# A selective-scan block and an expert network on one core: the convolution's weights and the first norm set up ahead of the other weights

## The chip, the core and the metric

The kernel runs on one core of a Trainium2 chip. A time is device microseconds (us) of one execution. The engines of the core work side by side and meet through semaphores: TensorE (PE, matmul; PEld is its weight load), VectorE (DVE), ScalarE (ACT), GpSimd (POOL), and SyncE (SP), which issues most of the DMAs.

## The reference, cut to what matters

For each of 32 sequences of 256 positions and 128 channels a selective scan is computed on the normed input, and then a gated network of 8 experts (the best 2 of 8 per position, 176 features each) and a shared part of 352 features:

```python
u = silu(conv4(W_in_u @ norm(x)) + conv_b)            # 256 channels, 4 taps
g = u @ W_gate.T                                      # 64 low-rank, 16 b, 16 c
delta = softplus(g[:64] @ W_delta.T + delta_bias)
h = exp(A * delta) * h + (delta * u) * b              # 256 channels x 16 states, along time
y = (sum(h * c) + D * u) * silu(o)                    # o = W_in_o @ norm(x)
x = x + y @ W_out.T
x = x + experts(norm(x)) + shared(norm(x))
```

## The kernel before, in words

**Steps.** All engines run the same loop of steps, k = -3 to 34 (`steps`, L309), each through its own `body`, which is an order written out by hand. A step works on several sequences at once; `on(lag)` says that sequence k + lag exists. In step k, sequence k + 3 is read and its mean and variance are taken; k + 2 is normed, transposed, convolved and gets its `u`, its `g` (L1044, copied to `g_sb` by L579) and `z` (L1083, copied to `z_sb` by L612); k + 1 gets softplus (L553), the products `dd` (delta in its one half by L563, delta times u in the other by L790) and the gate of the output (L513); k goes through the scan; k - 1 gets the second norm; k - 2 goes through the experts.

**The scan of one sequence.** The 256 x 16 states are 8 groups q = 0 to 7 of 128 partitions x 1024. SP spreads `dd` to four times as many partitions by eight DMAs (`rep`, L357, four for each half of the channels), and fetches `b` and `c` for all partitions (`bc`, L336) after a small store (`bc_rows`, L364). For each group ACT makes the decays with four exponentials (L489), POOL the `inject` (L410), DVE scans (L687), and then POOL, or DVE for groups 0 and 4 (L699), multiplies by c (`read`, L420), and PE sums the states (L894). Each of these is a queue of its own in fixed order, with waits on the others.

**Before the steps.** SP issues x of sequence 0 and 13 loads of weights, among them W_in, the taps, and four of 16-byte pieces for A_log (L325). DVE and PE wait for all of them; DVE scales W_in by the taps (L642), PE transposes that and the other weights (L866 to L875, 19 transposes), and DVE and ACT copy the results out, some as two parts, a rounded one and its rest (L650, L665). The transposed weights lie in `decay_ps`. Every engine waits for the last weight before its first `body`. ACT also issues the loads of the experts' weights (L457), into the tiles `state` and `read`, which the scan needs later; ACT rounds them (L534, L535) and DVE takes the rest (L793, L795), both inside step -1. POOL builds a selection matrix `csel_rows` in `rep0` (L388 to L393), which DVE copies (L645).

## Time and profile before

| | us |
|---|---|
| median of 3 runs | 1240.33 |
| the runs | 1239.35 to 1240.44 |
| profiled execution, its own time | 1238.7 |
| its span | 1237.0 |

Busy in the span: PE 1123.3 us (91%), POOL 1067.5 (86%), DVE 1066.9 (86%), ACT 1011.0 (82%). The page cuts the span into 40 slices of 31 us; all engines are at seven tenths or more from the third slice on, and below that in the first two. So the table tells of two things: a long stretch in which four engines share the load, and a start. A timeline row gives the start, the duration of the whole merged row, the engine, the line, the operation with its tiles, and in brackets the idle time before it with what ended it.

### The profile page before, as it was taken

The numbers are of one execution on the slowest core, as the hardware profiler recorded it, in microseconds if no ns is written. First come the engines' busy times: TensorE is split into PE (matmuls) and PEld (weight loads), VectorE is DVE, ScalarE is ACT, GpSimd is POOL, SyncE is SP. The second block draws the span as 40 slices with busy tenths as digits, with TensorE's granted clock in tenths as the row PEclk, the third lists the DMA queues.
The fourth block names the chain that finished last, engine by engine and source line by source line (L and its number), as shares of the span: only waits on it lengthen the run. The fifth ranks groups of instructions, "written<-read, shape, count | busy, mean of one in ns | idle before, by whom it ended". The sixth has DMA issues, their size and how long they took to land. (4 is left out here: it accounts for less than half of the span.)

```text
span 1237.0 us, 25691 instructions
## 1 busy us (share of the span) xinstructions
PE 1123.3 (91%) x9075; PEld 919.1 (74%) x9075; DVE 1066.9 (86%) x1700; ACT 1011.0 (82%) x2119; POOL 1067.5 (86%) x502
## 2 busy tenths in 40 slices
PE   3456999999999999999999999999999999998887
PEld 2334778878778787887787878877878788876676
DVE  3277899999999999999998999999999999999854
ACT  2778888888888888888988888889888988897642
POOL 3299899999999999999998999999999999999810
PEclk8767999999999999999999999999999999999899
DMA  4444433344434333444343334443433344434000
GB/s 119 109 111 105 102 84 85 107 109 109 99 92 112 87 82 101 109 109 113 79 113 86 82 101 109 108 112 80 113 94 83 93 109 110 107 79 103 5 6 9
DMA packets 71482, 115.05 MB, mean 93 GB/s; under 512 B 8174, under 2 KB 30395, under 8 KB 71355
## 3 DMA queue, kind: packets, MB, share of 16 engines
q1 hardware_dynamic: 67178, 110.71, 35.0%
q10 hardware_dynamic: 4176, 2.70, 0.8%
q8 instruction: 72, 1.18, 0.4%
q14 instruction: 56, 0.45, 0.1%
HBM read 41.04 MB, written 5.24 MB: 37 GB/s over the span
## 5 line engine op out<-in xcount | busy, mean ns | idle before, releaser
L410 POOL TENSOR_TENSOR inject<-rep,bc 128x1024 f32<-128x1024 f32 x256 | 604.6, 2384 | 20.2 <-DMA rep<-dd 20.2
L420 POOL TENSOR_TENSOR read<-state,bc 128x1024 f32<-128x1024 f32 x192 | 452.2, 2376 | 10.2 <-DVE state L687 8.8
L687 DVE TENSOR_TENSOR_SCAN state<-decay_ps,inject 128x1024 f32<-128x1024 f32 x192 | 432.0, 2279 | 13.8 <-ACT decay_ps L489 13.0
L489 ACT ACTIVATE decay_ps<-rep,neg_a 128x255 f32<-128x255 f32 x1024 | 427.0, 465 | 8.9 <-DVE state L687 3.5
L936 PE MATMUL acc_ps<-ffn_down,features 128*128 128x128 f32 (+1 forms) x1792 | 244.8, 281 | 0.5 <-DVE features L716 0.5
L936 PEld LDWEIGHTS acc_ps<-ffn_down,features 128*128 128x128 f32 (+1 forms) x1792 | 220.3, 192 | 23.4 <-DVE features L716 7.4
L902 PE MATMUL work_ps<-xn2T_part,ffn_gate 128*128 128x256 f32 x1344 | 219.4, 300 | 6.7 <-ACT g_silu L476 3.0
L476 ACT ACTIVATE g_silu<-work_ps 128x512 f32<-128x512 f32 x224 | 134.9, 602 | 105.4 <-PE work_ps L902 94.8
L902 PEld LDWEIGHTS work_ps<-xn2T_part,ffn_gate 128*128 128x128 f32 x1344 | 180.0, 193 | 52.1 <-ACT g_silu L476 22.7
L911 PE MATMUL work_ps<-xn2T_part,ffn_up 128*128 128x256 f32 x1344 | 193.2, 284 | 0.0
L708 DVE TENSOR_TENSOR features<-g_silu,work_ps 128x512 f32<-128x512 f32 x224 | 149.8, 682 | 47.8 <-PE work_ps L911 47.4
L911 PEld LDWEIGHTS work_ps<-xn2T_part,ffn_up 128*128 128x128 f32 x1344 | 174.0, 191 | 0.5
L687 DVE TENSOR_TENSOR_SCAN decay_ps<-decay_ps,inject 128x1024 f32<-128x1024 f32 x64 | 146.3, 2286 | 8.2 <-POOL inject L410 8.2
L894 PE MATMUL acc_ps<-read,sum_sel 128*32 128x256 f32 x1536 | 125.8, 404 | 29.3 <-POOL read L420 25.5
L716 DVE TENSOR_TENSOR features<-features,work_ps 128x512 f32<-128x512 f32 (+1 forms) x192 | 116.3, 632 | 22.6 <-PE work_ps L923 21.9
L1017 PEld LDWEIGHTS work_ps<-xnT_part,wconv 128*128 128x128 f32 x768 | 100.5, 203 | 28.9 <-ACT xnT_part L543 27.7
L1017 PE MATMUL work_ps<-xnT_part,wconv 128*128 128x256 f32 x768 | 107.2, 299 | 13.2 <-ACT xnT_part L543 13.2
L444 POOL TENSOR_TENSOR shift<-neg_mean,rstd 128x4 f32<-128x4 f32 x36 | 7.3, 202 | 101.5 <-ACT rstd L596 101.5
L894 PEld LDWEIGHTS acc_ps<-read,sum_sel 128*32 128x32 f32 x1536 | 30.9, 109 | 69.9 <-POOL read L420 53.4
L699 DVE TENSOR_TENSOR read_own<-decay_ps,bc 128x1024 f32<-128x1024 f32 x64 | 77.5, 1211 | 0.1
L923 PE MATMUL work_ps<-combT,csel 40*128 40x256 f32 x352 | 75.9, 315 | 1.3 <-DVE features L708 1.2
L923 PEld LDWEIGHTS work_ps<-combT,csel 40*128 40x128 f32 x352 | 49.2, 185 | 22.9 <-issue 12.4
(130 smaller groups left out, 1250.5 us busy)
## 6 DMA issues: line engine op xcount, KB each, us to landing
rep<-dd SPq DMA_DIRECT2D x256, 256.0 KB, 4.7
bc<-bc_rows SPq DMA_DIRECT2D x64, 512.0 KB, 4.6
x_in<-in_L_attn_x_dram SPq DMA_DIRECT2D x32, 128.0 KB, 2.1
out_dram<-result SPq DMA_DIRECT2D x32, 128.0 KB, 1.8
bc_rows<-g_sb SPq DMA_DIRECT2D x32, 32.0 KB
state<-in_L_ffn_w_gate_dram ACTq DMA_DIRECT2D x1, 704.0 KB, 4.4
read<-in_L_ffn_w_up_dram ACTq DMA_DIRECT2D x1, 704.0 KB, 5.9
ffn_down<-in_L_ffn_w_down_dram ACTq DMA_DIRECT2D x1, 704.0 KB, 7.2
```

Of the source, the lines that this page charges most:

```text
L410: pool.tensor_tensor(inject[:, at % RI], du_all, b_all, ALU.mult).then_inc(inject_done, 1)
L420: pool.tensor_tensor(read[:, at % RR], state[:, at % RS], c_all, ALU.mult).then_inc(read_done, 1)
L476: act.activation(g_silu[p % 2][:], banks[GATE_BANK[p]][:], ACT.Silu).then_inc(silu_done, 1)
L489: last = act.activation(decay_ps[:, at % 2, j, 1:T], rep[(HALVES * n + half) % RP][:, j, 0, 1:T], ACT.Exp, scale=neg_a[:, col:col + 1])
L687: dve.tensor_tensor_scan(to, decays, inject[:, at % RI].rearrange("p j t -> p (j t)"), 0.0, ALU.mult, ALU.add).then_inc(state_done, 1)
L708: dve.tensor_tensor(features[:, 2 * p:2 * p + 2, :].rearrange("p c t -> p (c t)"), g_silu[p % 2][:], banks[UP_BANK[p]][:], ALU.mult).then_ ...
L894: last = pe.matmul(y_ps[j * CB:(j + 1) * CB, :], sum_sel[:], products[:, j, :], start=False, stop=(g == SG - 1), skip_group_check=True)
L902: last = pe.matmul(banks[GATE_BANK[p]][:, side * T:(side + 1) * T], ffn_gate[w][:, chunk * P:(chunk + 1) * P], xn2T_parts[n % 2][d][:], st ...
L911: last = pe.matmul(banks[UP_BANK[p]][:, side * T:(side + 1) * T], ffn_up[w][:, chunk * P:(chunk + 1) * P], xn2T_parts[n % 2][d][:], start= ...
L923: last = pe.matmul(banks[COMB_BANK[i]][:, at * T:(at + 1) * T], csel[:, (chunk - NSH) * P:(chunk - NSH + 1) * P], combT[:], start=True, st ...
L936: last = pe.matmul(down_ps[:, j * DIM:(j + 1) * DIM], features[0:r, chunk, j * P:(j + 1) * P], ffn_down[0:r, chunk, :], start=fresh and j ...
L1017: last = pe.matmul(conv_ps[:, half * T:(half + 1) * T], wconv[w][:, half, tap, :], xnT_parts[d][:, tap:tap + T], start=(w + d + tap == 0), ...
```

## The change

- SP loads x, W_in and the taps, with a semaphore of their own (`conv_loaded`), then the other weights. The statistics of sequence 0 and its norm (step -3, and the start of step -2) come before or beside the scaling and transposing of the convolution's weights (`turn_conv`). The other weights are transposed in step -2, between the correction of x's transpose and the convolution (`turn_rest`), and ACT copies them there (`copy_weights`).
- The softplus of sequence 0 and its `dd` are made at the end of step -2, straight from `z_ps`; SP issues its `rep` in step -1. The first two groups of decays and the first three of `inject` of sequence 0 are made in step -1, in the middle of ACT's body and ahead of POOL's norm shift (`FIRST = 3`); `inject` 3 stays in step 0.
- The experts' weights are loaded by SP, behind `rep` of sequence 0, into `features` (the tile that held the weights' rows). Their rounding on ACT and the rest on DVE move from step -1 to step 1.
- `csel_rows` is built in `read`, after the norm shift of step -3. DVE copies it in step -1, and POOL waits for that copy before its first `read`.

```diff
+FIRST = 3
...
-        csel_rows = rep[0][:].rearrange("p b w t -> p (b w t)")[0:LOW + EXPERTS, 0:ROUTED]
-        gate_staged = state[:].rearrange("p b j t -> p (b j t)")[:, 0:PADDED]
-        up_staged = read[:].rearrange("p b j t -> p (b j t)")[:, 0:PADDED]
+        csel_rows = read[:].rearrange("p b j t -> p (b j t)")[0:LOW + EXPERTS, 0:ROUTED]
+
+        gate_staged = scratch[:, 0:PADDED]
+        up_staged = scratch[:, PADDED:2 * PADDED]
...
-        setup_loads = [
+        conv_loads = [
             (win_rows, W_in.rearrange("(c p) d -> p c d", p=P)),
             (taps[:], conv_w.rearrange("(c p) o k -> p c (o k)", p=P)),
+        ]
+        setup_loads = [
             (wgate_rows, W_gate),
             (wdelta_rows, W_delta.rearrange("(c p) r -> p c r", p=P)),
...
+            for to, source in conv_loads:
+                sp.dma_start(to, source).then_inc(conv_loaded, 16)
             for to, source in setup_loads:
                 sp.dma_start(to, source).then_inc(w_loaded, 16)
...
+                if k == -1:
+                    sp.wait_ge(turned, 2)
+                    for to, source in ffn_loads:
+                        sp.dma_start(to, source).then_inc(ffn_loaded, 16)
...
-                injects(1)
-                injects(2)
-                injects(3)
+                for q in (1, 2, 3):
+                    if k > 0 or q >= FIRST:
+                        injects(q)
+                if k == 0:
+
+                    pool.wait_ge(csel_ready, 1)
                 reads(1)
                 injects(4)
                 reads(2)
...
+                if k == -1:
+                    for q in range(FIRST):
+                        inject_group(0, q)
                 if on(3) or on(-1):
                     pool.wait_ge(ln_rstd, k + 4)
                     pool.tensor_tensor(shift[:], neg_mean[:], rstd[:], ALU.mult).then_inc(ln_shift, 1)
-                if on(1):
+                if on(1) and k >= 0:
                     inject_group(k + 1, 0)
                 reads(5)
                 reads(6)
...
-            act.wait_ge(w_loaded, 16 * len(setup_loads))
-            for to, source in ffn_loads:
-                act.dma_start(to, source).then_inc(ffn_loaded, 16)
...
+            def copy_weights():
+                act.wait_ge(turned, 2)
+                for half in range(HALVES):
+                    cols = slice(half * P, (half + 1) * P)
+                    act.copy(wg[:, half, :], turned_ps[:, 3, half * P:half * P + GATES]).then_inc(act_weights, 1)
+                    act.copy(wdelta[0:RANK, half, :],
+                             turned_ps[0:RANK, 3, (2 + half) * P:(3 + half) * P]).then_inc(act_weights, 1)
+                    act.copy(wo[0][:, half, :], turned_ps[:, 2, cols]).then_inc(act_weights, 1)
+                    act.copy(wout[:, half, :], turned_ps[:, 2, (2 + half) * P:(3 + half) * P]).then_inc(act_weights, 1)
+
+                act.wait_ge(weights_ready, EARLY_WEIGHTS)
+                act.activation(neg_a[:], turned_a, ACT.Exp).then_inc(prep_a, 1)
 
...
-                if on(2) or on(0) or on(-2):
+                if k >= -1 and (on(2) or on(0) or on(-2)):
...
-                if on(1) and not on(0):
+                if k == 1:
...
+                if k == -2:
+                    copy_weights()
+                if k == -1:
+
+                    act.wait_ge(weights_ready, WEIGHTS)
+                    decays(0, 0)
+                    decays(0, 1)
                 if on(0):
                     decays(k, 4)
-                if on(1):
+                if on(1) and k >= 0:
...
+                if k == -2:
+
+                    act.preload_act_table_set("softplus")
+                    act.wait_ge(z_mm, 1)
+                    act.activation(delta_ps, z_ps, ACT.Softplus).then_inc(delta_done, 1)
+                    act.wait_ge(delta_done, 1)
+                    act.copy(dd[:, :, 0, :], delta_ps).then_inc(dd_done, 1)
+                    act.copy(z_sb[:], z_ps).then_inc(z_copied, 1)
...
-                if on(1):
+                if on(1) and k >= 0:
                     decays(k + 1, 0)
                     decays(k + 1, 1)
 
-            steps(body)
+            step(body, -3)
...
+                if k == -2:
+
+                    dve.wait_ge(dd_done, 1)
+                    dve.tensor_tensor(dd[:, :, 1, :], delta_ps, u[0][:], ALU.mult).then_inc(du_done, 1)
+                if k == -1:
+                    dve.wait_ge(consts, 4)
+                    dve.tensor_copy(csel[:], csel_rows).then_inc(csel_ready, 1)
+                if on(1) and k >= 0:
                     n = k + 1
                     dve.wait_ge(delta_done, n + 1)
                     for half in range(HALVES):
                         dve.wait_ge(rep_in[half], 16 * JB * n)
                     dve.tensor_tensor(dd[:, :, 1, :], delta_ps, u[n % RU][:], ALU.mult).then_inc(du_done, 1)
...
-                if on(1) and not on(0):
+                if k == 1:
...
-            steps(body)
+            step(body, -3)
+            dve.wait_ge(conv_loaded, 16 * len(conv_loads))
+            for half in range(HALVES):
+                for tap in range(TAPS):
+                    dve.tensor_scalar(wconv_rows[:, half, tap, :], win_rows[:, half, :],
+                                      taps[:, half, tap:tap + 1], None, ALU.mult).then_inc(prep, 1)
+            dve.wait_ge(consts, 1)
+            dve.tensor_scalar(neg_identr[:], ident[:], -1.0, None, ALU.mult).then_inc(neg_ready, 1)
...
+            dve.wait_ge(turned, 1)
+            for half in range(HALVES):
+                dve.tensor_copy(wconv[0][:, half, :, :].rearrange("d k h -> d (k h)"),
+                                turned_ps[:, half, :]).then_inc(conv_ready, 1)
+            dve.wait_ge(conv_ready, HALVES)
+            for half in range(HALVES):
+                dve.tensor_tensor(wconv[1][:, half, :, :].rearrange("d k h -> d (k h)"), turned_ps[:, half, :],
+                                  wconv[0][:, half, :, :].rearrange("d k h -> d (k h)").bitcast(F32),
+                                  ALU.subtract).then_inc(conv_ready, 1)
+            dve.wait_ge(turned, 2)
+            dve.tensor_copy(conv_bias[:], turned_vectors[:, 0:HALVES]).then_inc(weights_ready, 1)
...
+            dve.wait_ge(prep_a, 1)
+            dve.tensor_scalar(neg_a[:], neg_a[:], -1.0, None, ALU.mult).then_inc(weights_ready, 1)
...
+            dve.wait_ge(weights_ready, WEIGHTS)
+
+            dve.memset(decay_ps[:, :, :, 0:1], 0.0).then_inc(decay_zero, 1)
+            steps(body, -2)
...
+            def turn_conv():
+                pe.wait_ge(consts, 1)
+                pe.wait_ge(prep, PARTS + 7 + HALVES * TAPS)
+                for half in range(HALVES):
+                    for tap in range(TAPS):
+                        last = pe.transpose(turned_ps[:, half, tap * P:(tap + 1) * P], wconv_rows[:, half, tap, :], ident[:])
+                last.then_inc(turned, 1)
+
+            def turn_rest():
+                pe.wait_ge(w_loaded, 16 * len(setup_loads))
+                pe.transpose(banks[0][:, 0:EXPERTS], router_rows, ident[0:EXPERTS, 0:EXPERTS])
+                pe.transpose(turned_vectors, vector_rows, ident[0:2 * HALVES, 0:2 * HALVES])
+                arows = HALVES * JB * SG
+                pe.transpose(turned_a, a_log_rows, ident[0:arows, 0:arows])
...
+                for half in range(HALVES):
+                    cols = slice(half * P, (half + 1) * P)
+                    pe.transpose(turned_ps[:, 3, half * P:half * P + GATES], wgate_rows[:, cols],
+                                 ident[0:GATES, 0:GATES])
+                    pe.transpose(turned_ps[0:RANK, 3, (2 + half) * P:(3 + half) * P], wdelta_rows[:, half, :], ident[:])
+                    pe.transpose(turned_ps[:, 2, cols], win_rows[:, HALVES + half, :], ident[:])
+                    last = pe.transpose(turned_ps[:, 2, (2 + half) * P:(3 + half) * P], wout_rows[:, cols], ident[:])
+                last.then_inc(turned, 1)
 
...
+                    if k == -2:
+                        pe.wait_ge(neg_ready, 1)
...
+                if k == -2:
+                    turn_rest()
...
+                    if k == -2:
+                        pe.wait_ge(conv_ready, PARTS * HALVES)
...
+                    if k == 2:
+                        pe.wait_ge(csel_ready, 1)
...
-            steps(body)
+            turn_conv()
+            steps(body, -2)
```

The places where the order of the queues moves. On ACT, around the first decays of sequence 0, before (L569 to L612 are sequence 1 in step -1; L494 opens step 0):

```order
L563 COPY dd<-work_ps 128x2x256 [waits rep_in1,rep_in0,du_done]
L569 ACTIVATE u<-work_ps,conv_bias 128x256 [waits sum_done,conv_mm]
L569 ACTIVATE u<-work_ps,conv_bias 128x256
L579 COPY g_sb<-work_ps 96x256 [waits z_mm,bc_out,g_mm]
L583 ACT_TABLE_LOAD
L593 ACTIVATE log_var<-mean_var,eps 128x4 [waits ln1_var,ln_shift]
L594 ACTIVATE neg_mean<-mean_var 128x4
L596 ACTIVATE rstd<-log_var 128x4 [waits ln_small]
L612 COPY z_sb<-work_ps 128x512 [waits z_mm,delta_done]
L489 ACTIVATE decay_ps<-rep,neg_a 128x255 [waits state_done,rep_in0]
L489 ACTIVATE decay_ps<-rep,neg_a 128x255 x3
```

The same place now (lines are those of the changed kernel; L517 is the decays, L606 `u` of sequence 1, L616 `g_sb`):

```order
L571 CAST xnT_part<-work_ps 128x256 [waits xnT_rest]
L517 ACTIVATE decay_ps<-rep,neg_a 128x255 [waits state_done,rep_in0,weights_ready]
L517 ACTIVATE decay_ps<-rep,neg_a 128x255 x3
L517 ACTIVATE decay_ps<-rep,neg_a 128x255 [waits state_done]
L517 ACTIVATE decay_ps<-rep,neg_a 128x255 x3
L590 ACT_TABLE_LOAD
L606 ACTIVATE u<-work_ps,conv_bias 128x256 [waits sum_done,conv_mm]
L606 ACTIVATE u<-work_ps,conv_bias 128x256
L616 COPY g_sb<-work_ps 96x256 [waits z_mm,bc_out,g_mm]
L628 ACT_TABLE_LOAD
L638 ACTIVATE log_var<-mean_var,eps 128x4 [waits ln1_var,ln_shift]
L641 ACTIVATE rstd<-log_var 128x4 [waits ln_small]
```

The decays stood behind everything of sequence 1 in step -1; now `u`, `g_sb`, the norm's small work and `z_sb` of sequence 1 stand behind the decays.

On POOL, around the first inject of sequence 0, before:

```order
L397 MEMSET read 128x32
L444 TENSOR_TENSOR shift<-neg_mean,rstd 128x4 [waits ln_rstd] x3
L410 TENSOR_TENSOR inject<-rep,bc 128x1024 [waits state_done,b_in,rep_in0]
L410 TENSOR_TENSOR inject<-rep,bc 128x1024 [waits state_done] x3
L420 TENSOR_TENSOR read<-state,bc 128x1024 [waits sum_done,state_done]
L410 TENSOR_TENSOR inject<-rep,bc 128x1024 [waits state_done,rep_in1]
```

and now (L458 is the shift, L418 the inject, L428 the read):

```order
L479 MEMSET features 128x32
L458 TENSOR_TENSOR shift<-neg_mean,rstd 128x4 [waits ln_rstd]
L418 TENSOR_TENSOR inject<-rep,bc 128x1024 [waits state_done,b_in,rep_in0]
L418 TENSOR_TENSOR inject<-rep,bc 128x1024 [waits state_done] x2
L458 TENSOR_TENSOR shift<-neg_mean,rstd 128x4 [waits ln_rstd]
L418 TENSOR_TENSOR inject<-rep,bc 128x1024 [waits state_done]
L428 TENSOR_TENSOR read<-state,bc 128x1024 [waits sum_done,state_done,csel_ready]
L418 TENSOR_TENSOR inject<-rep,bc 128x1024 [waits state_done,rep_in1]
```

Three injects stand ahead of the shift of step -1, and the fourth behind it.

## Rows read from the trace of the kernel before

**Rows 1.** The page's DMA issues: tiles, queue, count, KB each, us to landing.

```profile
x_in<-in_L_attn_x_dram SPq DMA_DIRECT2D x32, 128.0 KB, 2.1
```

**Rows 2.** Busy by stretch: length, PE, PEld, DVE, ACT, POOL, clock, DMA, GB/s.

```profile
157.00:194.00 37.00, 35.87 (x307) 29.05 (x306) 34.67 (x57) 32.38 (x70) 35.11 (x17) 1.00 0.36 95
```

**Rows 3.** Timeline of POOL, 55 to 91 us: start, us, what, idle before.

```profile
56.01 9.28 POOL L410 TENSOR_TENSOR inject<-rep,bc 128x1024 f32<-128x1024 f32 x4 [1.55 <-DMA rep<-dd]
...
83.95 6.96 POOL L420 TENSOR_TENSOR read<-state,bc 128x1024 f32<-128x1024 f32 x3
```

**Rows 4.** Timeline of SP, 0 to 57 us.

```profile
1.81 0.51 SPq L325 DMA_DIRECT2D taps<-in_L_attn_conv_w_dram  x1
...
35.97 1.26 SPq L336 DMA_DIRECT2D bc<-bc_rows  x2
37.27 0.59 SPq L346 DMA_DIRECT2D x_in<-in_L_attn_x_dram  x1
48.10 8.71 SPq L357 DMA_DIRECT2D rep<-dd  x8
```

**Rows 5.** Timeline of DVE, 0 to 22 us.

```profile
9.80 2.90 DVE L642 TENSOR_SCALAR features<-features,taps 128x128 f32<-128x128 f32 x8 [7.88 <-DMA features<-in_L_attn_A_log_dram]
...
16.73 1.29 DVE L650 CAST wconv<-decay_ps 128x512 fp32r<-128x512 f32 x2 [3.10 <-PE work_ps L875]
...
21.36 0.49 DVE L804 BATCH_NORM_STATS2 stats<-x_in 128x6 f32<-128x128 f32 x2
```

**Rows 6.** Timeline of PE: transposes and both convolutions of the prologue.

```profile
12.85 1.09 PE L866 MATMUL decay_ps<-ident,features 128*128 128x128 f32 x4 [12.85 <-DVE features L642]
...
27.23 4.37 PE L1017 MATMUL work_ps<-xnT_part,wconv 128*128 128x256 f32 x24 [0.46 <-ACT xnT_part L543]
...
44.31 5.49 PE L1017 MATMUL work_ps<-xnT_part,wconv 128*128 128x256 f32 x24 [2.86 <-ACT xnT_part L543]
```

**Rows 7.** Timeline of ACT, 23 to 46 us.

```profile
23.52 0.88 ACT L503 ACTIVATE xn<-x_in,shift,rstd 128x128 f32<-128x128 f32 x2 [0.32 <-POOL shift L444]
...
33.67 0.37 ACT L579 COPY g_sb<-work_ps 96x256 f32<-96x256 f32 x1 [1.19 <-PE work_ps L1044]
...
42.30 1.69 ACT L535 CAST ffn_up<-read 128x1792 fp32r<-128x1792 f32 x1
...
45.57 0.60 ACT L553 ACTIVATE work_ps<-z_sb 128x512 f32<-128x512 f32 x1
```

**Rows 8.** Timeline of ACT, 49 to 80 us: around the first decays.

```profile
49.84 0.84 ACT L569 ACTIVATE u<-work_ps,conv_bias 128x256 f32<-128x256 f32 x2 [1.76 <-PE work_ps L1017]
...
54.09 0.57 ACT L612 COPY z_sb<-work_ps 128x512 f32<-128x512 f32 x1
...
55.96 3.27 ACT L489 ACTIVATE decay_ps<-rep,neg_a 128x255 f32<-128x255 f32 x8 [1.31 <-DMA rep<-dd]
59.25 1.28 ACT L494 ACT_TABLE_LOAD   x1
60.54 0.88 ACT L503 ACTIVATE xn<-x_in,shift,rstd 128x128 f32<-128x128 f32 x2
...
63.22 1.67 ACT L489 ACTIVATE decay_ps<-rep,neg_a 128x255 f32<-128x255 f32 x4
...
78.03 1.67 ACT L489 ACTIVATE decay_ps<-rep,neg_a 128x255 f32<-128x255 f32 x4
```

**Rows 9.** Timeline of DVE: the scans of step 0 that wait for decays.

```profile
64.92 4.47 DVE L687 TENSOR_TENSOR_SCAN state<-decay_ps,inject 128x1024 f32<-128x1024 f32 x2 [0.46 <-ACT decay_ps L489]
...
79.73 6.65 DVE L687 TENSOR_TENSOR_SCAN state<-decay_ps,inject 128x1024 f32<-128x1024 f32 x3 [2.04 <-ACT decay_ps L489]
```

**Rows 10.** Timeline, all engines: a split in step -1, and step 1.

```profile
46.81 2.02 DVE L793 TENSOR_TENSOR ffn_gate<-state,ffn_gate 128x1792 fp32r<-128x1792 f32 x1
...
99.67 1.67 ACT L489 ACTIVATE decay_ps<-rep,neg_a 128x255 f32<-128x255 f32 x4 [0.24 <-DVE state L687]
...
107.94 0.42 DVE L722 TENSOR_TENSOR y_gated<-acc_ps,gate 128x256 f32<-128x256 f32 x1 [2.43 <-PE acc_ps L894]
```

133 lines of the change are left out of this document (52 added, 81 removed).

## The prediction, made before the changed kernel had run

> **What bounds the kernel now.** I read the busy time by stretch first. In a full step (157 to 194 us) PE is busy 35.9 us of 37, POOL 35.1, DVE 34.7 and ACT 32.4 [rows 2]: four engines in lock, each waiting for the others, so a steady step has no gap that a change to the start could fill or open. The change leaves these steps alone, apart from the first two. What is left is the start, and it is worth what it moves the scan of sequence 0 forward, less what it makes the first steps longer.
>
> I then read each engine's timeline of the first 60 us. POOL makes its first inject at 56.0 us, released by `rep` [rows 3], and has no gap from there to 90.9, the end of its step 0. What lies ahead of 56.0 is one chain. The eight scalings of W_in begin at 9.80, idle before them for 7.88 us on the load of A_log, though they need only W_in and the taps [rows 5]. 19 transposes on PE (12.85 to 16.7), then copies on DVE; the norm of sequence 0 begins only at 21.36, when all weights are done [rows 5, 6]; the normed x is out at 24.4, the convolution runs from 27.23, and `g_sb` is out at 34.04 [rows 6, 7]. Then step -1 does all of sequence 1 ahead of softplus: its second convolution, and two castings of the experts' weights (1.69 us the second) in front of it on ACT; softplus of sequence 0 starts at 45.57, `rep` is issued at 48.10 and lets POOL go 7.9 us later [rows 3, 4, 7].
>
> **Term 1: the weights of the convolution sooner.** The taps' DMA is issued at 1.81 with 0.51 of issue, and x's DMAs land 2.1 us after issue [rows 1, 4], so W_in and taps are there at 4.4 at the earliest, and at 9.8 at the latest, when everything was. I take 5.0, since x and W_in are all that stands ahead on the queue. The scalings take 2.90: 7.9. Eight transposes go at 1.09 us for four, overlapping: 1.9, to 9.8 [rows 5, 6]. The norm took from 21.36 to 24.40 [rows 5, 7]; from x's landing near 3 it is ready by 6, so its move ahead hides it beside the scalings. From the normed x to the convolution took 2.8 us (24.40 to 27.23), of which the last 0.4 is the copy of the low part; so at 12.2 PE is free for the other 11 transposes, 11/19 of 3.85 = 2.2 us: the convolution can start at 14.4. Its weights are copied and split on DVE by then (two casts 1.29 [rows 5], two subtractions of about the same: 9.8 to 12.6). ACT's eight copies, the exponential for A and the table load lie beside the convolution. From its start to the end of `g_sb` took 34.04 - 27.23 = 6.8: A = 21.2 instead of 34.04. Term: 12.8. Bounds: a convolution takes 4.4 us in the first and 5.5 us in the second case, at a lower clock [rows 6]; with the second A is 1.1 later, and if the clock has risen by then 1 to 2 earlier.
>
> **Term 2: softplus a step sooner.** From A: a table load 1.28, softplus 0.60, a copy of as much, DVE's product 0.7: `dd` is complete at A + 3.3 [rows 7, 8]. SP is not free: it issues `bc` from A + 1.93 for 1.26 us, and x for 0.59 [rows 4], so `rep` starts at A + 3.8 = 25.0. It let POOL go after 7.9 us, without anything else in flight. Now `bc` of 1 MB is in flight ahead of it; it was issued 12 us earlier before. Between no contention (0) and the whole overlap of 2.2 us I take 1.1. So the first half of `rep` lands at r = 34.0 instead of 56.0. Terms 1 and 2 together: 22.0 us.
>
> The Trainium skill speaks against part of this. Here a table load lasts 1.28 us and the next ACTIVATE starts 0.01 later, at 60.54 [rows 8]. Its page ScalarE: Activation LUTs, section What ACT_TABLE_LOAD costs, puts a switch at about 2.66 us, the load and a drain of about 1.38 with it. By that page the two table loads that this change puts on its path (this one, and one in term 3) would cost 2.8 us more, and the sum would be 11.2 instead of 14.0. The trace shows no drain, and the row decides.
>
> **Term 3: what the new order costs in steps -1 and 0.** The fourth inject and the third group of decays are the tender places. Before, ACT did the third group (L489 at 63.22) 7.3 us after r = 55.96. Now `u`, `g_sb` and `z_sb` of sequence 1 stand between: the stretch 49.84 to 54.66 = 4.8 us, and a table load more, 1.3: it comes at r + 13.4 [rows 8]. Scans 2 and 3 waited for exactly these decays at 64.92 = r + 9.0 [rows 9], so they come at r + 15.1. POOL does three injects (7.0), waits for the norm's work on ACT until about r + 9, does the shift and the fourth inject (to r + 11.5), a read and an inject, and then waits for scan 2 until r + 17.4; it had come through here at r + 13.9. In step 0 it then has two reads and three injects, and ends these at r + 29. On ACT softplus of sequence 1 goes later with its decays, its `u` and `g_sb` too, and so the sixth group of decays, before at 78.03 = r + 22.1, comes at about r + 27. The last three scans, which waited for it at 79.73 [rows 8, 9], are 5.0 later, and POOL's last read of step 0 with them. `rep` of sequence 1 is issued at r + 23.4 and lands at r + 31.3, a little after POOL wants it. POOL's step 0 ends 5.0 to 5.8 later after r than its 34.9 [rows 3]. Term: -5.5. Bounds: -3.6, the loss at POOL's second read, if the later groups of decays find gaps; -8.
>
> **Term 4: the experts' weights split in step 1.** Two casts on ACT of 1.69, 3.3 us with their overlap, now ahead of the decays of group 4 (at 99.67 in this step, which ran right into its scan); two subtractions on DVE, 2.02 each, after `dd`, where DVE next waited 2.43 us for PE until 107.94 [rows 7, 10]. So ACT's 3.3 us delay scan 4 and softplus; DVE's 4.0 lose about 2.4 in the gap, and what comes behind them (the statistics, group 4's read, the norm that xn2 needs) is 2.2 to 2.6 later at the end of the step. Below: 0, if both fall into gaps (POOL has none here, it is the other engines that do). Above: 7.3, all in series. I take -2.5, since the DVE gap is a row. What this costs step -1 before is already in the 22.0, as softplus stood behind the casts.
>
> **Edits at nothing.** The loads of the experts' weights on SP stand behind `rep` and are wanted in step 1, 40 us later; their cover is that whole step 0. Their rows of DMA stand ahead of `bc_rows` of sequence 1, which is wanted at r + 31: at the rate of `rep` (1 MB in under 7.9 us) the 2.6 MB and then `bc` are through at r + 26 even so. `csel`: POOL builds it after the shift of step -3, where it has nothing else to do, and DVE copies it while it waits for `rep`.
>
> **Sum.** 12.8 + 9.2 - 5.5 - 2.5 = 14.0. The profiled execution took 1238.7, so 1224.7; the median of the runs is 1.6 above it: 1226.3, say 1226.
>
> **Rivals.**
> A. More of the start is given back: term 3 at its bound of -8 and both splits nearly in series, -6. Then 22 - 14 = 8: 1232. For it: in step 1 ACT and DVE feed each other, and a scan waits on the decay that stands behind the casts. Against: DVE's gaps in this step.
> B. Less is given back: term 3 at -3.6, the splits at -1, the convolution at the raised clock (+1.5): 22 + 1.5 - 4.6 = 18.9, 1221. For it: PE works from 8 us on with few pauses. Against: the decays wait on a queue that has no slack.
> C. The other side: `rep` of sequence 0 lands late, as it now runs with `bc` in front, on a ring that the experts' loads follow. ACT's whole sequence 1 stands behind that landing. The change breaks even when terms 3 and 4 eat it up, that is at r = 56 - 8 = 48, so if `rep` takes 23 us from issue instead of 7.9. At 26 us it is 3 slower: 1243. Nothing in the rows comes near, as eight issues took 8.71 in all [rows 4].
> D. The change doesn't give what it says: the taps land with the last weights (at 9.8), so the convolution waits as before. Then 4.8 of term 1 is gone: 9 gained, 1231.
>
> The Trainium skill bears on C. In the rows the loads of the experts went by ACT's queue and nothing of SP's was wanted then. DMA: Bandwidth & Descriptors, section Queues, rings and completion order, says that an SDMA engine takes the descriptors of one ring in order. By that rule the loads can't slow `rep` ahead of them, only `bc_rows` behind; no run so far shows it.
>
> **Chances.** The forecast 0.62, with its own range 1222.5 to 1230; A 0.15, D 0.06, B 0.12, C 0.03, and 0.02 for a gain that vanishes. What a measurement can tell from no change is 0.2%, 2.5 us. Faster by more: 0.94; within: 0.03; slower: 0.03. The range for 8 in 10 takes in most of A, B and D: 1219 to 1232.5.
>
> **What would show it.** Scalings starting near 5 us on DVE; a first convolution from about 14.4, `g_sb` out near 21; `rep` issued near 25, and the first inject near 34. A gap of about 2 us on POOL between its third and fourth inject, and one before the second read; the third group of decays 13 to 14 us after the first. In step 1 the casts ahead of group 4's decays, and no idle of DVE where it had 2.43. POOL's end of step 0, before at 90.9, near 74.5; the same place of later steps 13 to 15 us earlier than before. It would be wrong if the first inject comes after 38, or if the steps from 2 on differ in length from those of before.

## The result, and the profile after

The forecast was 1226 us with a range of 1219 to 1232.5. Measured: 1233.71 us median (13 runs, 1227.76 to 1236.58) against 1240.44 for the kernel before (13 runs beside it); ratio 0.9936, 95% interval 0.9919 to 0.9954. The kernel is faster, by 6.7 us instead of 14, and the time lies 1.2 us above the range. The profiled execution took 1234.12 us, its span 1232.4 at a mean granted clock of 0.964. Three of the medians in the table of experiments (second run of the kernel after, e9, v4) count one execution each in a far slower state (2085, 3412 and 1772 us), which the ratios and their intervals leave out.

Places of the trace at which one reads where the gain is: the first inject, the start of the group of three injects that follows step 0 on GpSimd (rows 3 had its end of step 0 at 90.9), and GpSimd's tiny shift of steps 1 and 2, of which there is one per step.

| us | before | after | gain so far | forecast |
|---|---|---|---|---|
| first inject | 56.01 | 34.48 | 21.5 | 22.0 |
| end of step 0 | 90.88 | 74.69 | 16.2 | 16.5 |
| shift of step 1 | 114.09 | 105.44 | 8.65 | 14.0 |
| shift of step 2 | 150.71 | 141.83 | 8.9 | 14.0 |

So all that is missing up to here went in step 1. From there to step 18 the shifts of both kernels stay 8.5 to 9.1 apart; at the last shift they are 4.5 apart (see "Left open" below). GpSimd's rows for these places, before and after (a step ends where the next group of three injects starts, so step 1 took 32.6 us before and takes 40.2 after):

```profile
90.88 7.00 POOL L410 TENSOR_TENSOR inject<-rep,bc 128x1024 f32<-128x1024 f32 x3
114.09 0.19 POOL L444 TENSOR_TENSOR shift<-neg_mean,rstd 128x4 f32<-128x4 f32 x1
123.49 7.09 POOL L410 TENSOR_TENSOR inject<-rep,bc 128x1024 f32<-128x1024 f32 x3
```

```profile
74.69 7.01 POOL L418 TENSOR_TENSOR inject<-rep,bc 128x1024 f32<-128x1024 f32 x3
114.85 7.08 POOL L418 TENSOR_TENSOR inject<-rep,bc 128x1024 f32<-128x1024 f32 x3
141.83 0.20 POOL L458 TENSOR_TENSOR shift<-neg_mean,rstd 128x4 f32<-128x4 f32 x1 [1.25 <-ACT rstd L641]
```

The timeline of VectorE in the kernel after, prologue and step 1; it answers to [rows 5] and to the subtraction in [rows 10]:

```profile
3.06 0.49 DVE L822 BATCH_NORM_STATS2 stats<-x_in 128x6 f32<-128x128 f32 x2 [1.13 <-DMA x_in<-in_L_attn_x_dram]
...
4.57 5.93 DVE L878 TENSOR_SCALAR features<-features,taps 128x128 f32<-128x128 f32 x8 [0.75 <-DMA taps<-in_L_attn_conv_w_dram]
...
88.00 2.30 DVE L698 TENSOR_TENSOR_SCAN decay_ps<-decay_ps,inject 128x1024 f32<-128x1024 f32 x1 [2.12 <-ACT decay_ps L517]
90.21 0.68 DVE L808 TENSOR_TENSOR dd<-work_ps,u 128x512 f32<-128x512 f32 x1
90.80 9.02 DVE L811 TENSOR_TENSOR ffn_gate<-features,ffn_gate 128x1792 fp32r<-128x1792 f32 x1
99.74 2.01 DVE L813 TENSOR_TENSOR ffn_up<-features,ffn_up 128x1792 fp32r<-128x1792 f32 x1
```

Two durations are new. The eight scalings start early, at 4.57, but take 5.93 us where [rows 5] has 2.90 for the same work. And the first of two equal subtractions takes 9.02 us, the second 2.01, where [rows 10] has 2.02.

The timeline of GpSimd in the kernel after shows what it did meanwhile; it answers to [rows 3]:

```profile
4.85 1.26 POOL L469 MEMSET read<- 8x1408 f32 x1
6.19 1.35 POOL L471 TENSOR_SCALAR_AFFINE_SELECT read<-read 8x1408 f32<-8x1408 f32 x1
7.61 1.42 POOL L474 TENSOR_SCALAR_AFFINE_SELECT read<-read 8x1408 f32<-8x1408 f32 x1
...
34.48 7.02 POOL L418 TENSOR_TENSOR inject<-rep,bc 128x1024 f32<-128x1024 f32 x3 [6.34 <-DMA rep<-dd]
43.47 0.20 POOL L458 TENSOR_TENSOR shift<-neg_mean,rstd 128x4 f32<-128x4 f32 x1 [1.97 <-ACT rstd L641]
...
51.92 4.73 POOL L428 TENSOR_TENSOR read<-state,bc 128x1024 f32<-128x1024 f32 x2 [1.30 <-DVE state L698]
...
65.46 2.34 POOL L418 TENSOR_TENSOR inject<-rep,bc 128x1024 f32<-128x1024 f32 x1 [1.70 <-DMA rep<-dd]
...
86.28 4.75 POOL L428 TENSOR_TENSOR read<-state,bc 128x1024 f32<-128x1024 f32 x2
90.95 6.99 POOL L418 TENSOR_TENSOR inject<-rep,bc 128x1024 f32<-128x1024 f32 x3
105.44 0.20 POOL L458 TENSOR_TENSOR shift<-neg_mean,rstd 128x4 f32<-128x4 f32 x1 [7.50 <-ACT rstd L641]
```

The scalings ran beside the building of `csel`, and L811 ended 1.9 us after GpSimd's three injects, as if it had begun its 2 us of work only then. While GpSimd works, VectorE seems to stand still. Then GpSimd in turn waits 7.50 us for `rstd`, which waits for VectorE's statistics behind the subtractions. The Trainium skill has the rule, in its page SBUF — State Buffer, section Who interferes with whom: VectorE and GpSimd share a pair of SBUF ports, which a VectorE operation with two SBUF inputs needs against a GpSimd one that reads SBUF, and copies, casts and scalings can need in their two-port modes; who comes first holds it for the whole instruction. The prediction overlooked it. The experiments test it.

SP's and ACT's rows show nothing stretched: `rep` was issued at 26.90, the experts' loads behind it at 35.55, and the casts took 1.67 and 1.68 us in step 1. PE only waits longer (8.5 us in step 1 for VectorE's `y_gated`, which stands behind the subtractions).

### The profile page after: what moved, and what is told of

The parts are those of the page before. It is cut to its first block and busy times, and to the rows that moved or that the text cites. A ratio compares the mean times of both kernels' runs of the same rounds, so it can differ in the third digit from the quotient of the medians.

```text
span 1232.4 us, 25690 instructions
## 1 busy us (share of the span) xinstructions
PE 1128.1 (92%) x9075; PEld 924.1 (75%) x9075; DVE 1077.3 (87%) x1700; ACT 1006.8 (82%) x2117; POOL 1068.3 (87%) x502
## 5 line engine op out<-in xcount | busy, mean ns | idle before, releaser
L418 POOL TENSOR_TENSOR inject<-rep,bc 128x1024 f32<-128x1024 f32 x256 | 605.0, 2388 | 27.7 <-DMA rep<-dd 27.7
L428 POOL TENSOR_TENSOR read<-state,bc 128x1024 f32<-128x1024 f32 x192 | 452.8, 2380 | 14.7 <-DVE state L698 13.9
L517 ACT ACTIVATE decay_ps<-rep,neg_a 128x255 f32<-128x255 f32 x1024 | 425.4, 461 | 8.9 <-DVE state L698 3.2
L458 POOL TENSOR_TENSOR shift<-neg_mean,rstd 128x4 f32<-128x4 f32 x36 | 7.3, 202 | 80.7 <-ACT rstd L641 80.7
```

The lines of the kernel that those rows point to most:

```text
L418: pool.tensor_tensor(inject[:, at % RI], du_all, b_all, ALU.mult).then_inc(inject_done, 1)
L428: pool.tensor_tensor(read[:, at % RR], state[:, at % RS], c_all, ALU.mult).then_inc(read_done, 1)
L517: last = act.activation(decay_ps[:, at % 2, j, 1:T], rep[(HALVES * n + half) % RP][:, j, 0, 1:T], ACT.Exp, scale=neg_a[:, col:col + 1])
```

## The experiments

All kernels are edits of the kernel after. Times are set against the kernel before, run on the same chip. The first inject, the length of step 1 (from the end of step 0 to the next group of three injects) and the length from the end of step 0 to the shift of step 2 are read from GpSimd's timeline of the profiled execution.

| run | median us (runs) | ratio, 95% interval | first inject | scalings | first, second subtraction | step 1 | end of step 0 to shift of step 2 |
|---|---|---|---|---|---|---|---|
| before | | | 56.01 | 2.90 | 2.02, 2.02 in step -1 | 32.6 | 59.8 |
| after | 1233.71 (13) | 0.9936, 0.9919 to 0.9954 | 34.48 | 5.93 | 9.02, 2.01 | 40.2 | 67.1 |
| a1_after_again | 1233.38 (12) | 0.9929, 0.9902 to 0.9955 | 34.10 | 7.17 | 2.09, 4.16 | 36.2 | 61.7 |
| e1_csel_after_scaling | 1225.95 (6) | 0.9886, 0.9860 to 0.9912 | 31.95 | 1.67 | 2.08, 4.17 | 36.2 | 63.4 |
| e2_pool_yields | 1228.07 (6) | 0.9890, 0.9869 to 0.9910 | 33.94 | 5.94 | 2.08, 2.01 | 36.5 | 62.5 |
| e3_psum_input | 1228.28 (4) | 0.9918, 0.9891 to 0.9946 | 35.45 | 6.06 | 2.39, 2.40 | 34.4 | 60.8 |
| e4_pieces | 1232.41 (5) | 0.9935, 0.9903 to 0.9967 | 34.16 | 7.07 | 8.96, 2.42 | 40.5 | 67.0 |
| e8_later_04 | 1230.68 (4) | 0.9909, 0.9885 to 0.9934 | 35.12 | 6.06 | 3.92, 4.17 | 37.7 | 64.2 |
| e9_later_01 | 1230.06 (4) | 0.9904, 0.9866 to 0.9942 | 35.53 | 5.93 | 4.25, 4.17 | 37.7 | 63.9 |
| e7_old_order | 1236.78 (10) | 0.9961, 0.9939 to 0.9984 | 43.32 | 6.05 | 9.00, 2.01 | 40.2 | 67.0 |
| v1_split_early_only | 1224.17 (6) | 0.9864, 0.9832 to 0.9896 | 34.10 | 7.16 | in step -1 | 32.6 | 58.1 |
| v2_split_early | 1222.32 (6) | 0.9844, 0.9812 to 0.9875 | 29.51 | 1.66 | 2.02, 2.02 in step -1 | 32.6 | 59.1 |
| v4_first4 | 1219.98 (5) | 0.9827, 0.9798 to 0.9855 | 30.74 | 1.66 | in step -1 | 32.7 | 59.1 |
| v6_decays2 | 1223.06 (4) | 0.9852, 0.9824 to 0.9880 | 30.35 | 1.66 | in step -1 | 32.6 | 59.2 |

Step 1 alone is the cleaner of the two lengths: it is 32.6 or 32.7 us in the kernel before and in all four versions that have no split in it, where the longer one varies from 58.1 to 59.8 with GpSimd's waits in step 2.

**GpSimd waits until the scalings are done.**

```diff
             step(body, -3)
+            pool.wait_ge(prep, PARTS + 7 + HALVES * TAPS)
```

> GpSimd waits for VectorE's eight scalings of the prologue (L878) before it builds csel, so that nothing of GpSimd runs beside them. Theory (VectorE's two operands in SBUF stand still while GpSimd works in SBUF): the scalings take at most the 2.90 us that they took in the kernel before instead of 5.93, and the first inject starts 3 to 4 us sooner than in the kernel after (34.48 there, so about 31); the end of step 0 and all later steps move by as much, about 3 us less than the kernel after. Rival (the scalings are slow for another reason, such as the W_in rows arriving piece by piece): they take 5.9 us again, csel ends later, and the time is that of the kernel after.

VectorE's and GpSimd's timelines of this run, one row each:

```profile
4.47 1.67 DVE L879 TENSOR_SCALAR features<-features,taps 128x128 f32<-128x128 f32 x8 [0.66 <-DMA taps<-in_L_attn_conv_w_dram]
```

```profile
6.20 1.28 POOL L470 MEMSET read<- 8x1408 f32 x1 [1.31 <-DVE features L879]
```

Alone, the scalings take 1.67 us; even the 2.90 of before was stretched. `rep` is issued 3.9 us sooner (22.96), as expected, but takes 9.0 us to let GpSimd go instead of 7.6, so the first inject comes 2.5 us sooner; the rival falls. The median is 7.8 us below that of the kernel after, more than the 3 expected: the profile shows a shorter step 1 too (36.2 instead of 40.2), since the first subtraction did not wait here (below).

**GpSimd lets the subtractions through.**

```diff
+                if k == 1:
+                    pool.wait_ge(ffn_ready, PARTS)
                 injects(5)
```

> In step 1 GpSimd waits for both subtractions of the experts' low parts (L811 and L813) before its injects of sequences 5 to 7. Theory (L811's 9.02 us are 2.0 us of work and 7 us of standing still while GpSimd runs three injects): L811 takes about 2.0 us, the two end at about 95 instead of 101.7, the injects run from there to 102, and GpSimd's inject of the next step starts at about 111.4 instead of 114.85, 3.4 us less than the kernel after. Rival (the split's work itself stands in series on VectorE and costs what it costs, GpSimd has nothing to do with it): L811 takes 9 us again, GpSimd waits until 101.7 and the step ends 3 to 7 us later than in the kernel after.

VectorE's timeline, then GpSimd's:

```profile
90.82 2.08 DVE L813 TENSOR_TENSOR ffn_gate<-features,ffn_gate 128x1792 fp32r<-128x1792 f32 x1
92.83 2.01 DVE L815 TENSOR_TENSOR ffn_up<-features,ffn_up 128x1792 fp32r<-128x1792 f32 x1
```

```profile
94.92 6.96 POOL L418 TENSOR_TENSOR inject<-rep,bc 128x1024 f32<-128x1024 f32 x3 [3.90 <-DVE ffn_up L815]
101.84 0.20 POOL L460 TENSOR_TENSOR shift<-neg_mean,rstd 128x4 f32<-128x4 f32 x1
111.26 2.38 POOL L418 TENSOR_TENSOR inject<-rep,bc 128x1024 f32<-128x1024 f32 x1
```

As the theory has it, to 0.2 us: GpSimd stands 3.90 us and yet the step ends 3.6 us sooner than at 114.85. A wait of its own, on an engine that has no gap in this step, is cheaper here than the one it got. It is no cheaper than the taking of turns that other runs show below (36.5 against 36.2 us for step 1).

**One operand from PSUM, and its control.** In the first of the two runs the second operand is 256 columns of a PSUM bank; the control cuts the same pieces with both operands in SBUF. With the PSUM operand the low parts of the weights are not those of the reference, so that run is one for the times alone.

```diff
-                    dve.tensor_tensor(ffn_gate[1][:], gate_staged, ffn_gate[0][:].bitcast(F32),
-                                      ALU.subtract).then_inc(ffn_ready, 1)
...
+                    for staged, low in ((gate_staged, ffn_gate[1]), (up_staged, ffn_up[1])):
+                        for c in range(7):
+                            last = dve.tensor_tensor(low[:, c * 256:(c + 1) * 256], staged[:, c * 256:(c + 1) * 256],
+                                                     banks[0][:, 0:256], ALU.subtract)
```

> Changed computation: the two subtractions take their second operand from PSUM (256 elements of a bank, whatever they hold), in 7 pieces of 256 columns each, so the low parts of the experts' weights are not those of the reference. Everything else is as in the kernel after. Theory (only an operation with both operands in SBUF stands still beside GpSimd): no piece waits, each takes 0.3 to 0.4 us, the fourteen 4 to 6 us beside GpSimd's three injects, and GpSimd's shift comes at about 101 instead of 105.4. Rival (any VectorE access stands still, or the delay is one of the split's place): the first pieces together take 7 us or more, and the shift comes at 105 or later.

> The two subtractions of the experts' low parts in 7 pieces of 256 columns each, with both operands in SBUF as in the kernel after: the control of the run with a PSUM operand. Theory: the first piece stands still as long as GpSimd works, either until its current instruction ends (then a piece gets in between each two injects, 2.3 us apart, and the injects are little slower) or until all three injects are done (7 us for the first piece, 0.3 us for the others); either way the last piece ends near 102 and the shift comes at 105 to 106. Rival (the standing still comes from the length of the operation, or from its records): pieces of 0.3 us all through, and the shift at about 101.

VectorE's and GpSimd's timelines with the PSUM operand:

```profile
91.49 2.39 DVE L813 TENSOR_TENSOR ffn_gate<-features,work_ps 128x256 fp32r<-128x256 f32 x7
93.80 2.40 DVE L813 TENSOR_TENSOR ffn_up<-features,work_ps 128x256 fp32r<-128x256 f32 x7
```

```profile
91.63 7.02 POOL L418 TENSOR_TENSOR inject<-rep,bc 128x1024 f32<-128x1024 f32 x3
99.89 0.20 POOL L458 TENSOR_TENSOR shift<-neg_mean,rstd 128x4 f32<-128x4 f32 x1 [1.23 <-ACT rstd L641]
```

The view of line 813 in the control (ns: shortest, median, longest), and GpSimd's timeline:

```profile
L813 DVE TENSOR_TENSOR ffn_gate<-features,ffn_gate x7: 409/496/2570, 91.8 to 100.3; 128x256 fp32r<-128x256 f32 x7
L813 DVE TENSOR_TENSOR ffn_up<-features,ffn_up x7: 409/410/411, 100.7 to 102.7; 128x256 fp32r<-128x256 f32 x7
```

```profile
91.91 7.53 POOL L418 TENSOR_TENSOR inject<-rep,bc 128x1024 f32<-128x1024 f32 x3
106.76 0.20 POOL L458 TENSOR_TENSOR shift<-neg_mean,rstd 128x4 f32<-128x4 f32 x1 [7.32 <-ACT rstd L641]
```

With PSUM as a source both engines run side by side undisturbed: seven pieces take 2.39 us, as the control's second seven do alone (2.42), and the injects 7.02. With SBUF the first piece went through before the first inject, then three pieces of 0.41 us took 2.57 each, one behind each inject, and the injects 0.5 us more together. So it is the second SBUF operand, not the place, the length or the loads. The PSUM run also prices the split without contention: 34.4 - 32.6 = 1.8 us in step 1, of which 60.8 - 59.8 = 1.0 is left at the shift of step 2.

**The kernel after once more.**

> The kernel after, unchanged, once more, as the base of the other runs of this call and to see whether its stretched subtraction repeats. Theory (GpSimd in SBUF keeps VectorE's two-SBUF-operand subtraction waiting): L811 takes more than 4 us again and the eight scalings (L878) 5 to 6 us. Rival (an accident of the one profiled execution): L811 takes 2.0 us, and step 1 from shift to shift some 35 us instead of 41.9.

VectorE's timeline, then GpSimd's:

```profile
90.16 2.09 DVE L811 TENSOR_TENSOR ffn_gate<-features,ffn_gate 128x1792 fp32r<-128x1792 f32 x1
92.17 4.16 DVE L813 TENSOR_TENSOR ffn_up<-features,ffn_up 128x1792 fp32r<-128x1792 f32 x1
```

```profile
90.30 10.56 POOL L418 TENSOR_TENSOR inject<-rep,bc 128x1024 f32<-128x1024 f32 x3
100.81 0.20 POOL L458 TENSOR_TENSOR shift<-neg_mean,rstd 128x4 f32<-128x4 f32 x1
```

Neither the theory nor the rival is wholly right. The same program, with the subtraction issued at the same place to 0.02 us (0.21 us before GpSimd's read ended at 90.37, against 0.23 in the profile above), had another outcome: VectorE went first, and then the engines took turns, an inject for a subtraction. GpSimd's injects took 3.6 us more, and yet step 1 was 4.0 us shorter than in the first profile (36.2 against 40.2). This execution took 1227.24 us, near the forecast. The scalings' stretching did repeat.

**The subtraction issued a little later,** behind a small clearing on VectorE (352 columns; 4 in the second run).

```diff
+                    dve.memset(ffn_up[1][:, 0:352].bitcast(F32), 0.0).then_inc(ffn_high, 1)
+                    dve.wait_ge(ffn_high, PARTS + 1)
                     dve.tensor_tensor(ffn_gate[1][:], gate_staged, ffn_gate[0][:].bitcast(F32),
```

> The kernel after with one short clearing of 352 columns on VectorE ahead of the first subtraction of the experts' weights, so that L813 (L811 of the kernel after) is issued 0.4 us later, when GpSimd's first of three injects has begun, instead of 0.2 us before the end of its read. Three executions so far had the first subtraction at 9.0 us (GpSimd's three injects undisturbed, 6.99 us) and two at 2.1 us (the three injects at 10.56), with the issue within 0.04 us of the same place. Theory (which of the two gets its way is a close race at that boundary, and away from it they take turns): the first subtraction waits out one inject, 4.0 to 4.2 us, GpSimd's three injects take 9 to 11 us, step 1 takes some 37 to 39 us from shift to shift. Rival (VectorE that comes while GpSimd's queue is full waits for the whole row of injects): 8.6 us or more again, injects at 6.99, step 1 at 42.

> As the run before with 4 columns cleared instead of 352, so that the first subtraction is issued about 0.1 us later, still at or just before the end of GpSimd's read. Theory (a close race): either outcome, 2.1 or 9.0 us, or 4.1 as in the run with the longer delay; step 1 then 37, 42 or 38 us. Rival (the outcome is set by the kernel and not by some 0.1 us): the 9.0 us of the kernel after.

(The first text counts three executions at 9.0 us. A whole subtraction took that in two, the kernel after and the run with the old order; near it is only the control, whose first seven pieces took 8.96 us together, with a turn behind each inject.) VectorE's timeline of the run with 352 columns:

```profile
91.44 0.35 DVE L811 MEMSET ffn_up<- 128x352 f32 x1
91.83 3.92 DVE L813 TENSOR_TENSOR ffn_gate<-features,ffn_gate 128x1792 fp32r<-128x1792 f32 x1
95.66 4.17 DVE L815 TENSOR_TENSOR ffn_up<-features,ffn_up 128x1792 fp32r<-128x1792 f32 x1
```

Issued at the boundary (0.05 us before it, with 4 columns) or once the inject has begun, each subtraction waits for one inject, about 2 us, and GpSimd's three take 10.6 us, in both runs. So the outcome that cost 9.0 us belongs to an issue 0.2 us before the boundary between two GpSimd instructions, where it came twice (kernel after, and the old order, below) and turn-taking twice (second run of the kernel after, and csel later). Work added in front of the subtraction made the kernel no slower; the medians are 3.0 and 3.7 us lower, with intervals that overlap.

**The old order in steps -1 and 0.** The decays and the injects of the first groups go back behind the norm.

```diff
-                    if k > 0 or q >= FIRST:
-                        injects(q)
+                    injects(q)
...
-                if k == -1:
-                    for q in range(FIRST):
-                        inject_group(0, q)
...
```

> The kernel after with the order of before in steps -1 and 0 alone: the decays and injects of the first sequences are again issued at the end of step -1 behind the norm and GpSimd's shift, while the convolution, the first norm and the softplus stay early. The prediction put 5.5 us on this reordering as time given back. Theory: the first inject starts behind the shift of step -1, at about 41 to 43 instead of 34.5, the 34.9 us of the kernel before from first inject to the end of step 0 follow, so step 0 ends at 76 to 78 instead of 74.7, and the kernel is 1.5 to 3 us slower than the kernel after: the order's loss is worth taking. Rival (the new order gives back more than it brings): step 0 ends before 74, and the kernel is faster than the kernel after.

GpSimd's timeline:

```profile
43.17 0.20 POOL L454 TENSOR_TENSOR shift<-neg_mean,rstd 128x4 f32<-128x4 f32 x1 [15.13 <-ACT rstd L632]
43.32 9.28 POOL L418 TENSOR_TENSOR inject<-rep,bc 128x1024 f32<-128x1024 f32 x4
...
78.20 7.00 POOL L418 TENSOR_TENSOR inject<-rep,bc 128x1024 f32<-128x1024 f32 x3
```

From 43.32 to 78.20 are the 34.9 us of before; the kernel after needs 40.2 from its first inject, but starts 8.8 sooner. The order's loss of 5.3 buys 3.5 at the end of step 0. The medians differ by 3.1 and 3.4 us from the two of the kernel after, with intervals that overlap.

**The split moved into step -1,** on VectorE alone, while GpSimd waits for `rep`; without and with the later csel. More moves with it: SP loads the experts' weights in step -2, into `state` and `read`; csel is built in `rep0` and copied in step -2; the casts are VectorE's; and VectorE takes the statistics of the next sequence ahead of the split.

```diff
-                if k == 1:
...
+                if k == -1:
+                    dve.wait_ge(ffn_loaded, 16 * len(ffn_loads))
+                    dve.wait_ge(padded, 2)
+                    dve.tensor_copy(ffn_gate[0][:], gate_staged).then_inc(ffn_high, 1)
+                    dve.tensor_copy(ffn_up[0][:], up_staged).then_inc(ffn_high, 1)
                     dve.wait_ge(ffn_high, PARTS)
                     dve.tensor_tensor(ffn_gate[1][:], gate_staged, ffn_gate[0][:].bitcast(F32),
                                       ALU.subtract).then_inc(ffn_ready, 1)
...
```

> As the run before, with the experts' split in step -1, but csel built beside the eight scalings, as in the kernel after. Theory: the scalings take 5 to 6 us and the first inject starts at about 34.5, step 1 takes about 33 us from shift to shift, the time is about 1224 to 1226, 2.5 to 3 us more than with csel after the scalings. Rival (the scalings' delay is caught up before the first inject, or in step 0): both versions take the same time.

> The kernel after with the experts' split moved out of step 1: their weights are loaded by SP in step -2 into tiles that stand empty then, and VectorE does both casts and both subtractions in step -1 while GpSimd has nothing to do; and csel is built only after the eight scalings. Theory: the scalings take 1.7 us and the first inject starts at about 32, step 1 takes about 33 us from shift to shift instead of 41.9, the time is 1221 to 1223. Rival (the work is only moved, and costs in step -1 what it cost in step 1): VectorE's four operations there, about 8 us, push its first scan and the norm of the next step; the first inject starts at 32 but the end of step 0 comes 5 us or more later than in the kernel after, and the time is 1228 or more.

VectorE's timeline of the version with both, then GpSimd's:

```profile
4.55 1.66 DVE L874 TENSOR_SCALAR features<-features,taps 128x128 f32<-128x128 f32 x8 [0.77 <-DMA taps<-in_L_attn_conv_w_dram]
...
21.66 1.06 DVE L817 CAST ffn_gate<-state 128x1792 fp32r<-128x1792 f32 x1
22.64 1.08 DVE L818 CAST ffn_up<-read 128x1792 fp32r<-128x1792 f32 x1
23.76 2.02 DVE L820 TENSOR_TENSOR ffn_gate<-state,ffn_gate 128x1792 fp32r<-128x1792 f32 x1
25.70 2.02 DVE L822 TENSOR_TENSOR ffn_up<-read,ffn_up 128x1792 fp32r<-128x1792 f32 x1
31.99 2.30 DVE L692 TENSOR_TENSOR_SCAN decay_ps<-decay_ps,inject 128x1024 f32<-128x1024 f32 x1 [4.27 <-POOL inject L417]
```

```profile
21.72 1.06 POOL L457 TENSOR_TENSOR shift<-neg_mean,rstd 128x4 f32<-128x4 f32 x1 [6.81 <-ACT rstd L635]
29.51 7.00 POOL L417 TENSOR_TENSOR inject<-rep,bc 128x1024 f32<-128x1024 f32 x3 [6.73 <-DMA rep<-dd]
38.51 0.20 POOL L457 TENSOR_TENSOR shift<-neg_mean,rstd 128x4 f32<-128x4 f32 x1 [2.00 <-ACT rstd L635]
...
60.79 2.34 POOL L417 TENSOR_TENSOR inject<-rep,bc 128x1024 f32<-128x1024 f32 x1 [1.75 <-DMA rep<-dd]
```

All four operations end at 27.7, and 4.27 us of VectorE's idle time are left before the first scan. Steps 1 and 2 are as short as before, and the time is as expected: 11 us under the kernel after, for all these moves together. The two versions are 1.9 us apart in the medians, with overlapping intervals; the profiles have 4.6 us at the first inject and 3.3 at the shift of step 2. GpSimd's first row shows the standing still the other way round: a shift of 128x4 elements, elsewhere 0.20 us, took 1.06 beside VectorE's cast.

**Term 3 cut further:** a fourth inject ahead of the shift (`FIRST = 4`), and in the second run also the third group of decays behind the rstd of step -1.

> The version with the split in step -1 and csel after the scalings, with FIRST = 4: GpSimd issues four injects instead of three before the shift of step -1, where it waits 2.0 us for the norm's rstd. Theory (in steps -1 and 0 three waits of GpSimd make up term 3: 2.00 for rstd, 1.57 for a scan, 1.75 for the rep landing, 5.3 together): the first wait goes, the fourth inject ends about 0.3 us after it would have ended, and the wait for the scan grows from 1.57 to some 3.5 us since the decays of sequence 2 come no sooner; the gain is 0 to 1 us. Rival (GpSimd's order alone sets step 0): 2 us faster.

> As the run before, with the decays of sequence 2 of step 0 issued right behind the rstd of step -1 instead of behind the gate's silu of step 0, 4.6 us sooner. Theory (what is late in steps -1 and 0 is ScalarE, which serves both the norm and the decays): the scan of sequence 2 starts at about 41 instead of 44.8, GpSimd's wait for it goes, but the z copy, xn and the next softplus come 1.7 us later and the wait for the rep landing grows by as much; step 1's shift comes 0 to 2 us sooner than in the version with the split in step -1. Rival: the later softplus costs more than the scan brings, and the time is 1 to 2 us above it.

From the first inject to the shift of step 1 the three versions take 63.7, 63.7 and 63.5 us: GpSimd's wait for rstd is gone, and the next ones are longer (3.67 for the scan in the first run; 2.91, 0.99 and 1.23 for scan, rstd and `rep` in the second). So GpSimd's order does not set this length. ScalarE's work between the first inject and the second softplus may, but that is not shown: its decays moved forward in the second run gained nothing either. No gain over the split alone can be told: 0.9827, 0.9852 and 0.9844, with intervals that overlap. The best version is any of these three, 19 to 22 us (1.5 to 1.7%) under the kernel before.

## Why the prediction was wrong

**Terms 1 and 2 were right in sum,** 21.5 for 22.0, with two errors that nearly cancelled. W_in and the taps had landed by 4.57 (5.0), but the scalings took 5.93 instead of 2.90, so `g_sb` was out at 22.92 instead of 21.2. It followed that `rep` was issued at 26.90 instead of 25.0. `rep` itself made most of it good: 7.6 us from its issue to the first inject, not 9.0 (it did take 9.0 in the run with csel later). That part of the 22.0 was luck. The table load on this path took 1.28 us, and softplus began 0.02 later, at 24.23. The drain that the Trainium skill has behind it (page ScalarE: Activation LUTs, section What ACT_TABLE_LOAD costs) did not show.

**Term 3 was right:** 5.3 lost for 5.5, at the places named. The third group of decays starts at 47.85, 13.4 us behind the first as in the sum, and GpSimd waits 1.97 us for rstd, 1.30 for the scan and 1.70 for `rep`, 5.0 together; the run with the old order shows the trade.

**Term 4 failed:** "two subtractions on DVE, 2.02 each ... lose about 2.4 in the gap". The duration came from [rows 10], a subtraction in step -1 of the kernel before, when GpSimd stood idle ([rows 3]: its first inject is at 56.01). In step 1 GpSimd has work without a gap (before from 90.88 to 130.6, after from 74.69 until its three injects are done). The split cost 7.3 us (67.1 - 59.8) instead of 2.5; 1.0 of it is the work (PSUM run), 6.3 the standing still and the waits behind it. In step 1 alone it is 7.6, of which 1.8 is the work and 5.8 the standing still. Where the engines take turns the split costs 1.9 to 4.4 (61.7, 63.4, 63.9 and 64.2 in the table), and the gain at the shift of step 2 is 15.0, 15.1, 10.0 and 11.2 us, around the forecast of 14. The text ahead of the prediction has every engine at seven tenths or more from the third slice of the page on. That is not so: PE is at 5 and 6 tenths in the third and fourth. The start reaches to 124 us, and the split was moved within it, not out of it.

**"Edits at nothing" failed in one:** csel "after the shift of step -3, where it has nothing else to do". GpSimd had nothing else to do, but VectorE had, and what mattered was whose way it stood in: 3.9 us at the issue of `rep`, 2.5 at the first inject.

**Rival A** (1232, more given back) came near the time, with 8 us of term 3 and both splits "nearly in series" as its reasons. Term 3 came to 5.3, and the PSUM run, with the same casts and subtractions in the same place, prices the work at 1.0 to 1.8 and not 6: the number fits by chance. B (1221) needed a loss of 3.6 in term 3, where 5.3 came. C is out by the first inject at 34.48, D by the scalings at 4.57. That the kernel would be faster (0.94) was right.

**Left open.** How often the costly outcome comes, two profiles of the kernel after don't show. That it is the usual one is an inference: the first profiled execution (1234.12) lies at the median of its runs, the second (1227.24) 6 us below that of its own; and the run in which GpSimd lets the subtractions through has a median 5.6 us lower, with an interval that lies apart (0.9869 to 0.9910 against 0.9919 to 0.9954), though its step 1 would gain nothing on the taking of turns. Why a subtraction that misses the boundary stands through three injects, when one issued 0.2 us later stands through one, isn't settled; the rows of one engine overlap by up to 0.1 us, so the offsets are not known better than that.

Between shift 2 and the end the profiles differ by up to 7 us (1086.3 before, 1090.6 after, 1089.7 in its second, 1087.4 in the version with split and csel moved, 1093.0 in the one with the split alone). This goes in part with the granted clock of TensorE, which was 0.973 in a run of the csel edit with a span of 1218.9 us and 0.962 in one of 1228.7. In the first profile the gain falls from 8.7 to 7.1 us between the shifts of steps 18 and 19, and from 700 to 750 us the granted clock is 0.97, where the kernel before has 1.00. Over all runs listed the mean granted clock is 0.9679 before (47 runs, without one at 0.927) and 0.9654 after (24 runs); within either kernel 0.01 of clock goes with 6 to 8 us of span. So 1.4 to 2.1 us of the missing gain may lie there, an estimate from these runs. Whether the change lowers the clock, and why, no run tests.

## What to carry to other kernels

A duration read from a row holds for the company it had there. Before an operation is moved, ask what the engine that shares its path to memory does at the new place: VectorE's work with two SBUF operands, and its copies, casts and scalings within SBUF, belong where GpSimd waits for something anyway. And an engine that has "nothing else to do" is not free if what it does keeps a critical one waiting.

## What the hardware showed that was not expected

- VectorE and GpSimd hold each other up in both directions: a scaling of 0.28 us took up to 1.43 beside csel, a 2.0 us subtraction 4.2 or 9.0, a 0.20 us GpSimd operation 1.06, three injects 10.56 instead of 6.99. By the Trainium skill (SBUF — State Buffer, Who interferes with whom) the holder keeps the ports for one instruction; the runs agree in five profiles (four with whole subtractions, and the control in pieces), and disagree in two, where one subtraction waited out three GpSimd instructions.
- With its second operand in PSUM a VectorE subtraction ran beside GpSimd undisturbed (seven pieces in 2.39 us, 2.42 with GpSimd idle and both operands in SBUF).
- The early TensorE work comes in two speeds at a granted clock of 1.00 in both: the correction matmul took 0.55 us in the kernel after and 0.35 in its second run, and from VectorE's first copy of the convolution's weights to its copy of the router's took 4.4 and 3.3 us. Five of the thirteen profiles of the changed kernels have the faster one, among them both with the split moved and `FIRST = 3`, and neither with `FIRST = 4`; so the later first injects of those two (30.74 and 30.35 against 29.51) may come from this and not from the edit. The cause of the two speeds is open.
